# Softmax row sums of an attention and mixture-of-experts kernel: a transfer that transposes in place of a TensorE transpose

## What is computed

```python
att = jnp.einsum('bqhd,bkhd->bhqk', q, k) * scale
att = jnp.where(causal, att, -jnp.inf)
att = jax.nn.softmax(att, axis=-1)
y = jnp.einsum('bhqk,bkhd->bqhd', att, v)
...
return y @ w_out
```

## Time and profile before

| | |
|---|---|
| median of 3 runs | 983.83 us (982.76 to 984.08) |
| the profiled execution | 984.76 us, of which the span on the core 982.9 us |
| TensorE busy | 939.2 us, 96% of the span |
| VectorE, ScalarE, GpSimd busy | 70%, 68%, 36% |
| DMA, mean | 145 GB/s, 66,003 packets |
| granted TensorE clock, mean | 0.990 of full speed |

### The profile page before, as it was taken

How to read it: one execution, slowest core, us unless ns; L and a number is a source line. 1 busy time by engine, 2 the same in 40 slices (tenths; PEclk the granted TensorE clock), 3 DMA queues, 4 the chain that set the end, 5 groups by cost and what they waited for, 6 DMA issues and landing times.

```text
span 982.9 us, 20063 instructions
## 1 busy us (share of the span) xinstructions
PE 939.2 (96%) x7008; PEld 750.1 (76%) x7008; DVE 689.1 (70%) x2000; ACT 667.2 (68%) x1930; POOL 352.3 (36%) x349
## 2 busy tenths in 40 slices
PE   5679998999999999999999999999999999999998
PEld 3456776677788787878888887888878778777776
DVE  4789599576766657666575656666576786888884
ACT  3756767576767767676667766677766776677771
POOL 0231113463243243442434433435231444444441
PEclk9899999899999999999999999999999999999999
DMA  6497424462234435455253552547434542533321
GB/s 196 148 315 260 165 79 141 158 210 97 88 106 164 141 106 177 120 191 183 91 180 119 198 185 91 155 148 183 161 107 125 163 133 70 182 117 105 124 87 44
DMA packets 66003, 142.76 MB, mean 145 GB/s; under 512 B 7856, under 2 KB 40880, under 8 KB 64112
## 3 DMA queue, kind: packets, MB, share of 16 engines
q1 hardware_dynamic: 52896, 91.77, 28.3%
q0 software_dynamic: 12432, 49.29, 16.1%
q10 hardware_dynamic: 576, 0.42, 0.2%
HBM read 104.76 MB, written 36.70 MB: 144 GB/s over the span
## 4 chain that ended last, share of the span: by engine, by line
PE 83%; issue 7%; DVE 4%; POOL 2%; DMA 2%; ACT 1%; SPq 0%; POOLq 0%; DVEq 0%
PE PS L674 15%; PE PS L675 14%; PE PS L722 14%; PE PS L676 14%; PE PS L713 14%; PE PS L703 9%; PE PS L697 2%; DMA xr<-in_w_moe 2%; PE PS L830 2%; POOL hh L1376 1%; DVE acc L1004 1%; DVE pp L1263 1%; POOL rstd L1368 1%; PE PS L728 1%; DVE acc L1180 0%
## 5 line engine op out<-in xcount | busy, mean ns | idle before, releaser
L943 ACT ACTIVATE pp<-pp,nmax 128x128 f32<-128x128 f32 (+3 forms) x512 | 281.0, 553 | 92.0 <-DVE nmax L1263 91.4
L1263 DVE CUSTOM_DVE_ANT_0 pp<-PS,maskw 128x128 f32<-128x128 f32 (+3 forms) x512 | 215.1, 484 | 4.4 <-PE PS L703 2.6
L1424 POOL TENSOR_TENSOR yy<-yf,yy 128x512 fp32r<-128x512 f32 x63 | 81.5, 1293 | 275.6 <-ACT yy L871 275.2
L713 PE MATMUL PS<-ident,pp 128*128 128x128 f32 x1280 | 165.0, 276 | 0.1
L713 PEld LDWEIGHTS PS<-ident,pp 128*128 128x128 f32 x1280 | 141.0, 140 | 15.0 <-issue 9.9
L722 PE MATMUL PS<-pt,vv 128*64 128x512 f32 (+3 forms) x1024 | 152.0, 439 | 0.0
L722 PEld LDWEIGHTS PS<-pt,vv 128*64 128x64 f32 x1024 | 67.9, 136 | 90.2 <-issue 73.3
L703 PE MATMUL PS<-qk 64*128 64x256 f32 (+2 forms) x1152 | 123.7, 354 | 3.4 <-ACT pt L871 1.6
L871 ACT ACTIVATE pt<-PS 128x384 f32<-128x384 f32 (+1 forms) x215 | 109.0, 514 | 2.7 <-PE PS L713 2.7
L1269 DVE COPY pt<-PS 128x384 f32<-128x384 f32 x169 | 99.2, 592 | 11.1 <-PE PS L713 10.8
L1418 POOL TENSOR_TENSOR hh<-hf,hh 128x256 fp32r<-128x256 f32 (+1 forms) x55 | 49.6, 901 | 146.1 <-ACT hh L871 145.9
(11 more groups left out here) (171 smaller groups left out, 2124.0 us busy)
## 6 DMA issues: line engine op xcount, KB each, us to landing
rb<-rr_scratch SPq DMA_DIRECT2D x128, 128.0 KB
wr<-wm_scratch SPq DMA_DIRECT2D x16, 768.0 KB, 5.8
y_scratch<-acc SPq DMA_DIRECT2D x39, 256.0 KB
acc<-in_x SPq DMA_DIRECT2D x15, 512.0 KB, 5.5
wm_scratch<-hh SPq DMA_DIRECT2D x10, 768.0 KB, 4.0
xs_scratch<-wr SPq DMA_DIRECT2D x7, 1024.0 KB, 5.2
xs<-xs_scratch SPq DMA_DIRECT2D x7, 1024.0 KB
xn_scratch<-acc SPq DMA_DIRECT2D x8, 512.0 KB, 3.3
```

The source lines that it names most:

```text
L713: done = e.transpose(o, pp[:, i % 4, P_AT[t] + 128 * kt:P_AT[t] + 128 * kt + 128], ident[:, :])
L943: e.activation(scores, scores, ACT.Exp, scale=-1.0, bias=nmax[:, b, t:t + 1], accum_out=rs[:, i % 4, 2 * t + h:2 * t + h + 1]).then_inc(a_ ...
L1263: e.tensor_tensor_reduce(pp[:, b, P_AT[t]:P_AT[t] + n], g[:, at:at + n], maskw[:, 512 - n:512], -1.0, 3e38, ALU.add, ALU.min, accum_out=nm ...
L1424: e.tensor_tensor(yy[:, i % 2, 1, :], yf[:, :], f32(yy[:, i % 2, 0, :]), ALU.subtract).then_inc(g_yl, 1)
```

## The change

The reciprocals go from `rr` straight to `rr_scratch`, whose layout is now tile, head, query. The destination is written so that partition q's eight numbers go to eight places 512 B apart. TensorE's transpose, its PSUM bank, ScalarE's copy and `rrT` are gone. The tick that followed `recip_rows` is gone too, for each pair. On SyncE's queue the transfer stands at tick lag 0 and waits for the reciprocals; it used to stand at lag 6 and wait for ScalarE's copy. The transfers back keep lag 7 and read four runs of 128 numbers where they read one of 512. VectorE may overwrite `rr` when the transfer of four pairs before has landed.

```diff
 HELD = {"finish": 57, "scores": 2, "transposes": 3, "attend": 3, "query": 1, "key": 2, "value": 4, "gate_up": 3,
-        "out_part": 1, "down": 3, "recip_rows": 3, "block_rows": 4}
+        "out_part": 1, "down": 3, "block_rows": 4}
...
         if P == NHT // 2 - 1:
             put("recip_rows", P)
-            tick()
...
                 if not h and P < NHT // 2 - 1:
                     put("recip_rows", P)
-                    tick()
...
-        rrT = sb("rrT", [8, 2, 128])
...
-        rr_d = nc.dram_tensor("rr_scratch", [4, 2, 4, 128], F32)
+        rr_d = nc.dram_tensor("rr_scratch", [4, 4, 2, 128], F32)
...
-            "recip_rows": lambda P, _: (a_rb, P + 1),
...
-                elif kind == "recip_rows" and lag == LAG["rr"]:
-                    w.wait_ge(a_rb, i + 1)
-                    e.dma_start(rr_d[i % 4].rearrange("h t q -> t h q"), rrT[:, i % 2, :]).then_inc(d_rr, 16)
+                elif kind == "recip_rows" and lag == 0:
+                    w.wait_ge(v_rr, i + 1)
+                    e.dma_start(rr_d[i % 4].rearrange("t h q -> q (t h)"), rr[:, i % 4, :],
+                                allow_slow_non_contiguous=True).then_inc(d_rr, 16)
...
-                        e.dma_start(rb[64 * h:64 * h + 64, :],
-                                    rr_d[i % 4, h:h + 1].rearrange("h t q -> h (t q)").to_broadcast([64, 512])
+                        e.dma_start(rb[64 * h:64 * h + 64, :].rearrange("p (t q) -> p t q", t=4),
+                                    rr_d[i % 4, :, h:h + 1, :].rearrange("t h q -> h t q").to_broadcast([64, 4, 128])
                                     ).then_inc(d_rb, 16)
...
-                elif kind == "recip_rows":
-                    w.wait_ge(v_rr, i + 1)
-                    w.wait_ge(*free)
-                    e.transpose(g[0:8, 0:128], rr[:, i % 4, :], ident[:, :]).then_inc(p_rb, 1)
...
-                elif kind == "recip_rows" and lag == 0:
-                    w.wait_ge(p_rb, i + 1)
-                    if i >= 2:
-                        w.wait_ge(d_rr, 16 * i - 16)
-                    copy(rrT[:, i % 2, :], bank(kind, i, j)[0:8, 0:128]).then_inc(a_rb, 1)
...
                     if i >= 4:
-                        w.wait_ge(p_rb, i - 3)
+                        w.wait_ge(d_rr, 16 * i - 48)
                     e.reciprocal(rr[:, i % 4, :], rs[:, i % 4, :]).then_inc(v_rr, 1)
```

More of the change, by code:

```diff
@@ L330, in attention_moe_kernel @@
             new_sem("p_" + n) for n in ("xt", "lgt", "lgc", "tot", "tk", "lat", "q", "k", "v"))
[L331 to L335, removed]
+        p_S, p_T, p_PV, p_out, p_fin, p_bt, p_gu, p_dn = (
+            new_sem("p_" + n) for n in ("S", "T", "PV", "out", "fin", "bt", "gu", "dn"))
+        a_whi, a_xth, a_lgr, a_sig, a_lat, a_q, a_k, a_v, a_exp, a_pt, a_yh, a_wo = (
+            new_sem("a_" + n) for n in ("whi", "xth", "lgr", "sig", "lat", "q", "k", "v", "exp", "pt", "yh",
                                         "wo"))
```

## The result

The changed kernel took 1206.01 us in the median of four runs (1202.62 to 1210.25), the kernel before 983.51 us beside it (982.76 to 984.08). The ratio is 1.227, with a 95% interval of 1.225 to 1.229. The forecast was 976.5 us.

A forecast was written before the change was run, and what follows sets the result against it. TensorE, busy 96% of the span, was taken as the bound; 5.7 + 0.3 + 1.4 = 7.4 us off 984.76 gives 977.4, lowered 0.93 to the median level: 976.5 us. Own range 973 to 980, with rivals 971 to 986.

The forecast's parts named there:

- The store's price: Transfer of the sums, 1,024 packets of 4 B at 55 ns each: 5.2 us to landing (3.4 to 14.4).
- the forecast gain of 1.4 us: Tail: without the last transpose TensorE skips its 1.29 us wait for reciprocals plus a 0.11 us slot.
- What hides it: Transfer issued 7 us earlier, landing 3.4 us later, so broadcasts no later; DMA share rising to about 0.76 costs nothing.
- The sentence on what is late next: If the transfer takes beyond about 9 us, VectorE's normalisation is late next, then the projections reading its result.
- So the queue doesn't stand at it, save in the tail: SyncE's queue: reciprocals come early, so the transfer's wait for them doesn't hold the queue except in the tail.
- The ticks: One tick less per pair shifts routing work against TensorE's, 100 to 220 us: counted nothing, 5 us either side.
- The removed transposes: TensorE, 64 transposes fewer: 5.7 us saturated stretch, 0.3 us between 100 and 150 us, 1.4 us tail; 7.4 us gained.
- The broadcasts at 0.6 to 1.3 us more: Broadcasts read 512 B runs instead of 2 KB: 24 more packets per engine and pair, 26 to 55 ns each.
- ScalarE's copies at nothing: Removing 64 copies, 16 us in all, from ScalarE gains nothing, since it has free time in each stretch.
- The rule of the Trainium skill: Rearranged plain transfer 19 times slower; if applied to the old 1.8 us: 34 us per transfer, kernel over 2,000 us.
- Expert weights late: Rival: small packets delay expert-weight loads, stalling TensorE 10 to 24 us; about 990 us, chance 0.12.
- DMA engines full: Rival: from 108 ns per packet DMA engines fill; at 150 ns, 140 us longer, 1,115 us; chance 0.06.

The follow-up runs named there:

- the store alone, unread: Kernel before plus the number-by-number store of adjacent numbers into a tensor nobody reads: 1154.48 us beside 982.69, ratio 1.174.
- the natural store with ticks: Changed kernel with sums stored as 128 runs of 32 B (divisors in wrong order) and tick put back: 984.67 us (ratio 0.986), then 978.48 (0.996).

## Why the prediction was wrong, step by step

- **The store's price** failed first. The step read: "I take 55 ns, the row of mostly small packets", 5.2 us to landing. It measured 8.2 us alone and 11 to 12 us in the pairs looked at in the kernel (10.6 to 15.5 where it lies on the chain). The size is off by two, but the model was wrong, not only its number: the rows that I priced from hold packets whose targets don't touch, and for such targets even the lowest bound is enough (2.7 us for 1,024 packets 512 B apart, where 26 ns gives 3.4 and 55 ns 5.2). The adjacent 4 B writes take 8.2 us although their packet records last 7 ns each, so no price for a packet could have given it. In the tail the forecast gain of 1.4 us turned into a loss: TensorE, which stood for 1.29 us, now stands for 6.09 us until `yf` is split.
- **What hides it: "That is below full, and I count it at nothing for the sum"** is the step that cost most. From 250 us on the share rose to 0.64 to 0.67, less than my 0.76, and was not near full; only between 50 and 125 us was it. Still the store alone, unread, cost 172 us, where the whole change cost 222. In place of nothing, loads land later (GpSimd's after 10.1 us in the median instead of 6.1) and SyncE's queue stands behind its own small store (334.3 us). The engines' busy share doesn't show this.
- The sentence on what is late next held for the normalisation: beyond 9 us it came late (76.5 us of waits of VectorE). TensorE then stood first at the transposes (L710, 41.4 us), not at the projections that I had named. From the unread store to the changed kernel with its ticks, which adds reader and wait and takes the transposes away, the ratio goes from 1.174 to 1.196, 2%, with the uncertainty named above.
- "So the queue doesn't stand at it, save in the tail", said of the wait for the reciprocals, was wrong: SyncE's queue stands there for 127.9 us (29 waits) in the changed kernel and for 191.3 us (39 waits) in the natural store with ticks. The latter is still faster than the kernel before, so this error cost little by itself.
- **The ticks: "I take nothing, and 5 us to either side".** They cost 16 us alone, and some 1 to 3% of the time before on top of the store (1.227 against 1.196, or against 1197.1/983 = 1.218). Nothing is lost between 100 and 200 us, where I had looked; the loss is from 50 to 100, from 200 to 250, and most of it from 750 us on.
- **The removed transposes: 7.4 us.** They gave 5.8 us against the kernel without the tick and 4.5 against the kernel before. Right in kind; they gave a fifth to two fifths less than forecast. That fits the distance of two starts as the price of a slot, of which a part comes back as new small gaps (the natural store with ticks has TensorE busy for 249.16 of 250 us from 250 us on, and 248.49 from 500 us on, where the earlier trace rows have 734.81 of 735).
- The broadcasts at 0.6 to 1.3 us more: some 0.5 measured, just below. About 65,000 more packets below 512 B: 66,304, right. ScalarE's copies at nothing: nothing speaks against it, not tested by itself.
- **The rivals.** "Expert weights late" happened (31.7 and 19.6 us on loads of `wr`, a median to landing beyond the 8.6 us that I had named as a sign), but with 990 us it was far too small. "DMA engines full", with 0.06, came nearest in size, 1,115 us, 132 of the 222 us; its mechanism did not come from 250 us on. One was tied to 1.1 us more for each load, the other to 108 ns for a packet; with a packet at 55 ns I had set both aside.
- **The rule of the Trainium skill.** In "DMA: Bandwidth & Descriptors", "Rules for kernel authors", the factor for a rearranged plain transfer is 19 against the hardware's transpose, which no run here has. Set against the contiguous store, as the prediction did, it measured 6.7 alone. The direction was right and the price from my rows was not; 2,000 us was far too much. The Trainium skill says in the same page, in "Specifications", that below 512 B the DMA does read-modify-write. That writes which share a block would then wait for one another is my inference, and not stated there; the 8.2 us for adjacent numbers agree with it, but the cost is gone at 32 B already, where every write is still below 512 B, and no run here shows the mechanism itself.

What the experiments show: the loss comes from the closeness of the written numbers, not from their count, nor mainly from the wait for them. Not shown: that adjacent writes wait for one another, which is only the reading that fits best, and the size of a block in which they would. One column of 128 numbers takes 7.2 us and eight columns side by side 8.2, as if separate blocks went on in parallel; blocks of 64 B and of 512 B would both roughly fit the times by distance. But the same addresses, 8 B apart, took 5.3 or 4.3 us with the numbers dealt out otherwise, and 256 numbers took longer than 1,024 (8.5 to 9.3 us), which neither size explains.

## What to carry to other kernels

Price a transfer by where its pieces land, not only by their number: a transposing store of 4 B numbers to adjacent DRAM addresses is to be measured by itself, with a load behind it, before it goes into a kernel. A DMA share below full is no proof of room; look at the times to landing of the transfers around it. And when an edit removes a slot from a hand-tuned order, run the removal of the slot alone: here it cost 16 us, about three times what the removed work was worth.

## What was not expected of the hardware

- 1,024 numbers written 4 B apart: 8.2 us; 8 B: 4.3; 16 B: 3.0; 32 B: 2.9; 512 B: 2.7. 128 adjacent numbers take 7.2 us (6.5 in another round), while 128 adjacent runs of 32 B take 1.4.
- A load of 512 KB behind the adjacent store on the same queue: 12.6 instead of 3.3 us. On another queue, in the kernel with the unread store: 10.1 instead of 6.1 us in the median for 768 KB.
- In the tail 1,040 packets are recorded within 1 us, and the completion comes 12.1 us after the issue: the packet records of this store end long before it has landed.
- Number by number is cheap when it reads DRAM: 2.3 us for 1,024 numbers, 3.4 from the natural layout.
